# Attention scores from three bf16 parts instead of two float32r parts, with the 4-bit weight tables made during the attention

## The reference, cut to what matters

```
qkv = hidden_states @ Wqkv                     # 32 query heads of 16, one key head, one value head
scores = einsum('bqhd,bkd->bhqk', q, k) / 4 + slope[h] * (pos_k - pos_q)   # causal, else -1e30
attn = softmax(scores) @ v, then @ Wo
# feed-forward: gate, up (512 x 1376) and down (1376 x 512) are 4-bit codes:
w = scales[g_idx[k], n] * (code[k, n] - (zero[g_idx[k], n] + 1))
y = (silu(x @ gate) * (x @ up)) @ down
```

## Time and profile before

| | |
|---|---|
| median of 3 runs | 1397.24 us (1396.83 to 1401.67) |
| the profiled execution's own time | 1395.92 us |
| its span | 1394.1 us |
| mean granted clock of TensorE | 0.956 of full speed |
| busy: PE, weight loads, DVE, ACT, POOL | 1239.7, 826.8, 730.3, 571.8, 308.0 us |
| last instruction of the attention on POOL | issued at 747.83 us |
| first instructions of the feed-forward block | 753.37 us |
| first gate matmul | 799.73 us |

### The profile page before, as it was taken

How to read it: one execution, slowest core, us unless ns; L and a number is a source line. 1 busy time by engine, 2 the same in 40 slices (tenths; PEclk the granted TensorE clock), 3 DMA queues, 4 the chain that set the end, 5 groups by cost and what they waited for, 6 DMA issues and landing times. The chain is left out here.

```text
span 1394.1 us, 16630 instructions
## 1 busy us (share of the span) xinstructions
PE 1239.7 (89%) x6208; PEld 826.8 (59%) x6208; DVE 730.3 (52%) x1353; ACT 571.8 (41%) x1006; POOL 308.0 (22%) x329
## 2 busy tenths in 40 slices
PE   4599999999999999989992389999999999579995
PEld 4567456555554656544541257778778788346664
DVE  4376785786688887723214666342141210365553
ACT  5143455265456565556661344311111111034443
POOL 0121141111110101011124344411121111115554
PEclk9999999899999999999996599999999999889998
DMA  6534223201221012122001422230020010130303
GB/s 194 112 54 113 43 40 106 40 2 39 47 56 25 23 19 40 25 40 40 18 31 51 124 72 62 94 106 0 0 91 1 0 61 1 59 105 1 121 0 120
DMA packets 60942, 75.97 MB, mean 54 GB/s; under 512 B 14738, under 2 KB 37530, under 8 KB 60796
## 3 DMA queue, kind: packets, MB, share of 16 engines
q1 hardware_dynamic: 57252, 64.42, 18.7%
q0 software_dynamic: 2560, 8.39, 1.7%
q10 hardware_dynamic: 1056, 2.16, 0.4%
HBM read 53.46 MB, written 21.59 MB: 54 GB/s over the span
## 5 line engine op out<-in xcount | busy, mean ns | idle before, releaser
L792 DVE TENSOR_REDUCE mx<-bank 128x1 f32<-128x512 f32 (+2 forms) x576 | 367.3, 685 | 138.7 <-PE bank L910 85.1
L734 ACT ACTIVATE PT<-ST 128x512 f32<-128x512 f32 x576 | 313.3, 600 | 210.3 <-PE ST L975 90.0
L907 PE MATMUL bank<-KS,QS 126*128 126x512 f32 (+2 forms) x896 | 253.3, 365 | 18.1 <-DMA QS<-pos_scratch 15.8
L975 PE MATMUL ST<-QS,KS 128*128 128x512 f32 x576 | 240.1, 457 | 5.0 <-DMA QS<-mparts 4.1
L907 PEld LDWEIGHTS bank<-KS,QS 126*128 126x128 f32 x896 | 158.7, 197 | 82.9 <-DVE mx L792 37.7
L975 PEld LDWEIGHTS ST<-QS,KS 128*128 128x128 f32 x576 | 108.3, 195 | 82.6 <-ACT PT L734 64.1
L989 PE MATMUL PO<-PT,V 128*32 128x512 f32 x1152 | 152.2, 604 | 1.6 <-ACT PT L734 1.6
L51 PE MATMUL f_pair<-f_xT,gu 128*128 128x512 f32 (+1 forms) x352 | 142.1, 404 | 0.0
L1495 DVE TENSOR_TENSOR f_h<-f_h,f_pair 128x512 f32<-128x512 f32 (+1 forms) x44 | 30.2, 686 | 210.1 <-ACT f_h L1402 210.1
L53 PE MATMUL f_pair<-f_xT,gu 128*128 128x512 f32 (+1 forms) x352 | 139.8, 397 | 0.0
L52 PE MATMUL f_pair<-f_xT,gu 128*128 128x512 f32 (+1 forms) x352 | 139.4, 396 | 0.0
(11 more groups left out here) (181 smaller groups left out, 1777.6 us busy)
## 6 DMA issues: line engine op xcount, KB each, us to landing
QS<-q_scratch SPq DMA_DIRECT2D x48, 256.0 KB
q_scratch<-QP SPq DMA_DIRECT2D x24, 256.0 KB, 2.3
l_x<-x_dram SPq DMA_DIRECT2D x12, 512.0 KB, 4.2
xres<-_attn_hidden_states_dram POOLq DMA_DIRECT2D x16, 256.0 KB, 3.0
x_dram<-xout POOLq DMA_DIRECT2D x16, 256.0 KB, 2.4
f_xin<-x_dram SPq DMA_DIRECT2D x4, 1024.0 KB, 7.0
f_xsum<-x_dram SPq DMA_DIRECT2D x4, 1024.0 KB, 6.9
x_dram<-f_xsum SPq DMA_DIRECT2D x4, 1024.0 KB, 4.8
```

The costliest lines, as they stand in the source:

```text
L734: act.activation(PT[:, quad % PT_RING, n % 4, :], ST[:, n % ST_RING, :], ACT.Exp).then_inc(p_done, 1)
L792: v.tensor_reduce(mx[:, i % 2, z, h:h + m], at(u).rearrange("p (m k) -> p m k", m=m), AX.X, ALU.max).then_inc(bank_free_dve, 1)
L907: last = pe.matmul(at(u)[:, j * w:(j + 1) * w], hi(QS[0:ROWS1, slot, h + j, :]), hi(KS[b][0:ROWS1, k0:k0 + w]), start=(j == 0 or not diag) ...
L975: last = pe.matmul(dst, hi(KS[b][0:ROWS2, kb * P:(kb + 1) * P]), hi(QS[0:ROWS2, slot, h:h + 4, :]), start=True, stop=not diag)
```

## The change

Scores now come from bf16 operands. A float32 value is split in three bf16 parts; of the nine pairings six are kept (`Q_PART`, `K_PART`), so `KS` and `QS` hold 6 x 16 = 96 rows of parts, 6 rows of positions (key number split in two exact bf16 parts, slope in three), zeros, and 3 rows for three parts of the maxima. The two rows that subtracted slope times the block's first position, the same for a whole softmax row, are dropped. All of p1, tiles and masks are now bf16; projections, `values` and everything behind are as before. The second part is made by ACT from a float32 rest (`second_part`), the third on POOL for queries (`query_low`) and on DVE for keys and maxima (`keys_done`, `max_done`). The rest of a query tile lives in one of two halves of `qrest`, so DVE waits until POOL has read the one two tiles back. `q_scratch` is bf16 (runs of 256 bytes where they were 512), and a block's stack is six DMAs of half the size each. `k_scratch` and `pos_scratch` are gone. `PT` has five slots instead of three.

Second, `plan_order` gets work of its own for the feed-forward part from block 10 on: POOL clears and fetches table inputs (`clear_tables`, `fetch_tables`), DVE makes the tables and unpacks the first two code units, ACT splits the scales, PE turns the one-hot matrices ("dt"), and a sixth piece (`AFTER`) loads the first 512 rows of the attention's own output, normalizes and turns them into the `xT` that `ffn` uses. The buffers are laid out ahead in `program`. `ffn` starts with the six early pieces at once. The plan's costs change with it (`p1` and `tile` 232 to 218, new kinds of work, store and maxima delays longer).

```
-POS = slice(3 * HD, 3 * HD + 2)
-ROWS1 = P - 2
+PARTS = 3
+Q_PART = (0, 0, 0, 1, 1, 2)
+K_PART = (0, 1, 2, 0, 1, 0)
+SETS = len(Q_PART)
+POS = slice(SETS * HD, SETS * HD + 2 * PARTS)
+ROWS1 = P - PARTS
...
-PT_RING = 3
+PT_RING = 5
...
+AFTER = NC
+PIECES.append((0, 0, 4))
...
+            if u == maxima_of(AFTER_AT)[0]:
+                sp_issue(("load", AFTER), e)
+                pend["pool"].append((("clear",), e))
+                for k in range(CODE_RING):
+                    sp_issue(("codes", k), e)
...
-        q_scratch = nc.dram_tensor("q_scratch", (B, QB, 2, 4, HD, P // HD, P), F32).ap()
-        pos_scratch = nc.dram_tensor("pos_scratch", (1 + QB, 2, NH, P), F32).ap()
-        k_scratch = nc.dram_tensor("k_scratch", (ROWS2 - POS.start, S), F32).ap()
+        q_scratch = nc.dram_tensor("q_scratch", (B, QB, PARTS, 4, HD, P // HD, P), BF16).ap()
...
-        KS = [sb(f"KS{b}", [P, S]) for b in range(B)]
+        KS = [sb(f"KS{b}", [P, S], BF16) for b in range(B)]
-        QS = sb("QS", [P, QSLOTS, NH, P])
+        QS = sb("QS", [P, QSLOTS, NH, P], BF16)
+        mparts = sb("mparts", [NH, 2, PARTS, P], BF16)
...
-                for part, ready in enumerate((q_hi_done, q_lo_done)):
+                for part, ready in enumerate((q_hi_done, q_mid_done, q_lo_done)):
...
-                for g, part in enumerate((0, 0, 1)):
+                for g, part in enumerate(Q_PART):
-                sp.dma_start(QS[POS.stop:POS.stop + 2, slot, :, :], pos_scratch[qb]).then_inc(qs_in[slot], 16)
...
+                elif kind == "codes":
+                    if i == 0:
+                        full(sp, ("kv", NC - 1))
...
+            def query_low(k, m):
+                pool.wait_ge(q_mid_done, 4 * k + m + 1)
+                n = PIECES[k][2] * P
+                pool.tensor_tensor(QP[:, 2, m, cols_of(k)], qrest[:, m % 2, 0:n], QP[:, 1, m, cols_of(k)], ALU.subtract).then_inc(q_lo_done, 1)
+
+            def clear_tables():
+                full(pool, ("kv", NC - 1))
+                pool.wait_ge(q_out, Q_OUT * NC)
+                pool.memset(dq.zpacked, 0).then_inc(cleared, 1)
+                pool.memset(dq.s_raw, 0.0).then_inc(cleared, 1)
+                pool.memset(dq.tables, 0.0).then_inc(cleared, 1)
+                pool.memset(dq.ztab, 0.0).then_inc(cleared, 1)
+
+            def fetch_tables():
+                for dst, src in table_loads:
+                    pool.dma_start(dst, src, allow_slow_non_contiguous=True).then_inc(ids_in, 16)
+                pool.wait_ge(cleared, 4)
+                for m in range(3):
+                    g0, g, w = FIRST_GROUP[m], GROUPS_OF[m], D if m == 2 else INTER
+                    for i in range(3):
+                        pool.dma_start(dq.s_raw[i * G_ROWS + g0:i * G_ROWS + g0 + g, 0:w], mats[m][1]).then_inc(s_in, 16)
+                    pool.dma_start(dq.zpacked[g0:g0 + g, 0:w // PACK], mats[m][2]).then_inc(z_in, 16)
+
             piece_rstd(0)
...
+            def second_part(u):
+
+                kind, k = u[0][:-1], u[1]
+                freed(act, (kind, *u[1:]))
+                if kind == "q":
+                    m, n = u[2], PIECES[k][2] * P
+                    act.activation(QP[:, 1, m, cols_of(k)], qrest[:, m % 2, 0:n], ACT.Copy).then_inc(q_mid_done, 1)
+                elif kind == "kv":
+                    n = PIECES[k][2] * P
+                    act.activation(kpart[:, 1, 0:n], krest[:, 0:n], ACT.Copy).then_inc(k_mid_done, 1)
+                else:
+                    act.activation(mparts[:, k % 2, 1, :], mrest[:, k % 2, :], ACT.Copy).then_inc(m_mid_done, 1)
...
+                    if rest_before(u):
+                        _, kb, mb = rest_before(u)
+                        v.wait_ge(q_lo_done, 4 * kb + mb + 1)
+                    v.scalar_tensor_tensor(qrest[:, m % 2, 0:PIECES[k][2] * P], at(u)[:, 0:PIECES[k][2] * P], HD ** -0.5, QP[:, 0, m, cols_of(k)],
+                                           ALU.mult, ALU.subtract).then_inc(bank_free_dve, 1)
...
+            def keys_done(k):
+                b, t, n = PIECES[k]
+                v.wait_ge(k_mid_done, k + 1)
+                v.scalar_tensor_tensor(KS[b][0:SETS * HD, t * P:(t + n) * P], kpart[:, 1, 0:n * P], gmask[0:SETS * HD, 1:2], krest[:, 0:n * P],
+                                       ALU.mult, ALU.add).then_inc(ks_ready, 1)
+
+            def max_done(i):
+                v.wait_ge(m_mid_done, i + 1)
+                v.tensor_tensor(mparts[:, i % 2, 2, :], mrest[:, i % 2, :], mparts[:, i % 2, 1, :], ALU.subtract).then_inc(m_lo_done, 1)
...
-                    last = pe.matmul(at(u)[:, j * w:(j + 1) * w], hi(QS[0:ROWS1, slot, h + j, :]), hi(KS[b][0:ROWS1, k0:k0 + w]),
+                    last = pe.matmul(at(u)[:, j * w:(j + 1) * w], QS[0:ROWS1, slot, h + j, :], KS[b][0:ROWS1, k0:k0 + w],
...
+                elif kind == "dt":
+                    n = min(4, DQ_COLS - u[1])
+                    act.wait_ge(cleared, 4)
+                    act.activation(dq.onehotT[0:S_ROWS, u[1]:u[1] + n, :], at(u)[0:S_ROWS, 0:n * P].rearrange("p (u k) -> p u k", k=P),
...
-                last = pe.matmul(dst, hi(KS[b][0:ROWS2, kb * P:(kb + 1) * P]), hi(QS[0:ROWS2, slot, h:h + 4, :]), start=True, stop=not diag)
+                last = pe.matmul(dst, KS[b][0:ROWS2, kb * P:(kb + 1) * P], QS[0:ROWS2, slot, h:h + 4, :], start=True, stop=not diag)
...
-    uses = [("dq", 0, j) for j in EARLY_PIECES] + [("xt", 0, t) for t in range(4)]
+    uses = [("dq", 0, j) for j in EARLY_PIECES]
...
-            sp.dma_start(xin[:, :, :], rows(x1_dram, 0)).then_inc(x_in, 16)
-            sp.wait_ge(cleared, 2)
-            for m in range(3):
-                g0, g, w = FIRST_GROUP[m], GROUPS_OF[m], D if m == 2 else INTER
-                sp.dma_start(zpacked[g0:g0 + g, 0:w // PACK], mats[m][2]).then_inc(z_in, 16)
-                for i in range(3):
-                    sp.dma_start(s_raw[i * G_ROWS + g0:i * G_ROWS + g0 + g, 0:w], mats[m][1]).then_inc(s_in, 16)
-            sp.wait_ge(tables_done, 2)
-            for u in range(len(UNITS)):
-                load_codes(u)
-                if u == 2 * CODE_RING + 2:
-                    sp.wait_ge(turned, 4)
-                    sp.dma_start(xin[:, :, :], rows(x1_dram, 1)).then_inc(x_in, 16)
+            sp.dma_start(xin[:, :, :], rows(x1_dram, 1)).then_inc(x_in, 16)
+            for u in range(CODE_RING, len(UNITS)):
+                load_codes(sp, mats, dq, u)
...
-            for u in range(CODE_RING):
-                codes(u)
-            row_moments(0)
-            normalize(0)
...
-            pe.wait_ge(onehot_done, 1)
-            for a in range(DQ_COLS):
-                if a == 16:
-                    pe.wait_ge(onehotT_done, 1)
-                pe.matmul(turn[:, a // 4 % 4, a % 4 * P:(a % 4 + 1) * P], onehot[:, a, :], identb[:, :], start=True, stop=True).then_inc(onehot_turned, 1)
-            pe.wait_ge(onehotT_done, -(-DQ_COLS // 4))
-            pe.wait_ge(tables_done, 2)
             for j in EARLY_PIECES:
                 weight_piece(j)
-            for t in range(4):
-                transposes(0, t)
```

More of the change, by code:

```diff
@@ L10 @@
+from collections import namedtuple
 from contextlib import ExitStack
@@ L177, in sp_issue @@
             free["sp"] = t + 300
+        elif j[0] == "codes":
+            free["sp"] = t + 2400
+            end["codes", j[1]] = t + 6000
         else:
@@ L871, in _ @@
             v.wait_ge(consts_in, 32)
-            for u in FIRST:
+            for u in FIRST[:-1]:
                 take(u)
+            keys_done(0)
+            take(FIRST[-1])
             for u in ORDER["dve"]:
@@ L939, in fill @@
                         last = pe.transpose(dst[:, t * P:(t + 1) * P], kvf[:, t * P:(t + 1) * P], ident[:, :])
+                elif kind == "dt":
+                    pe.wait_ge(onehot_done, 1)
+                    for k in range(min(4, DQ_COLS - u[1])):
+                        last = pe.matmul(dst[0:S_ROWS, k * P:(k + 1) * P], dq.onehot[:, u[1] + k, :], identb[:, :], start=True, stop=True)
                 elif kind == "mt":
```

562 lines of the change are left out of this document (321 added, 241 removed).

## The result

The changed kernel takes **1317.36 us** (median of 4, 1314.54 to 1319.98) against 1397.75 of the kernel before, measured beside it: a ratio of **0.9419** (95% interval 0.9387 to 0.9452), about 81 us faster. The direction was right and the place of the hole too; the attention's share was sized at half of what it is. Rival 2, "all of it is realized", named 1316.

A forecast was written before the change was run, and what follows sets the result against it. PE was taken to bound the attention, DVE second, followed by a 46.4 us hole. Span 1394.1 - 24.5 (attention) - 29.6 (hole) = 1340.0 us, giving a forecast of 1343 us, range 1318 to 1372.

The forecast's parts named there:

- the hole: Between attention and first feed-forward gate matmul: 46.4 us shrinks to 16.8, -29.6 us, including a new 5.5 us wait for codes.
- the attention's share: Attention: -29.5 us from scores, plus 3 for its start and 2 for maxima, -24.5 us in all.
- Rival 2: All score savings realized, loads vanish wholly, deeper ring helps: 1316 us; chance 0.17 for below 1327 us.
- uncovered weight loads: Scores, behind 128-column masks and values quads: bf16 halves the exposed loads, 12.5 us saved, bounds nothing and 25.
- 128-key banks: Score segments of 128: a matmul falls from 0.103 to 0.07 us, 8.5 us saved, bounds 1.0 and 12.8.
- I take 80%: Attention: of 41.5 us PE savings 80% is realized, 33 us, as DVE rises above 90% and strict queues lose some.
- Rival 1: Attention: score gain eaten by DVE and new links, only the gap before feed-forward pays: 1370 us; chance 0.18.
- The additions: New work in the attention: 3.6 us on PE, 3 for longer chains at the start, 2 for maxima.
- block 1's first p1 near 73 us: Start of the attention: sign expected in the profile after, with longer chains adding 3 us, bounds -2 and 8.
- The ring: Attention: the deeper PT ring only loosens ACT while PE is full: 0 us, bounds -5 and 0.
- Rival 3: Query stores before blocks 0 and 1: shorter runs make stores take twice as long, 1348 us; chance 0.08.
- Rival 4: Attention: DVE waits for POOL at query rests and table steps, PE stops, slower, 1413 us; chance 0.04.

The follow-up runs named there:

- the streams: Extra unread matmul streams behind the last output projection, in the kernel before (float32r) and the changed kernel (bf16); for example 128 columns took 0.112 and 0.056 us.
- e1: Kernel before with bf16 score operands and nothing else (scores less accurate): 1335.57 us, ratio 0.9562.
- e8: Changed kernel with three of the six stack loads, and so three of the six products, left out: 1311.93 us, ratio 0.9365.
- e16: Changed kernel storing two of three query parts, the second used in place of the third: 1314.40 us, ratio 0.9396.
- e2: Kernel before with bf16 score operands and a PT ring of 5 instead of 3: 1332.08 us, ratio 0.9529.
- e15: e2 with the changed kernel's planner costs for score matmuls, normalization and store delays: 1337.73 us.
- e3: Changed kernel with a PT ring of 3 instead of 5: 1315.22 us, ratio 0.9405.

## Why the prediction was wrong

The step that failed is the term for **uncovered weight loads**, with the one for 128-key banks. I wrote "a bf16 load is half as long, so I take half of both: 12.5 us", bounds 0 and 25. By the streams the parts of the cycles and quads beyond the plain rate are 128 x (0.103 - 0.022) + 144 x (0.131 - 0.022) = 26.1 us: nearly all of it went, a little more than my upper bound of 25. What counts is whether the load still shows behind the columns ahead of it, not how much shorter it is. Only the mask of 128 leaves 0.008 uncovered (0.277 against 0.216 + 0.053). The 128-column term gave 14.3 instead of 8.5: I took 0.070, and the stream runs at 0.056, although its load is shown as 0.099 in the earlier trace rows; and the float32r stream runs at 0.112, not 0.103. (The price is the stream's; in place, with a 512-column mask between, it may be some 2 us less in all.) In the other direction 512 columns gave 0.011 instead of 0.016, 12.5 us with the diagonal tiles instead of 15.4, and 256 columns 3.1 instead of 5.1. The sum is 56 instead of 41.5, inside my bounds of 21.5 to 58 but far from my middle.

The second failed step is "I take 80%". PE's busy share in the middle is 98 to 99% at the new rate, with DVE at 84 or 90%, and `e1` shows the whole rate term in the time. Rival 1, which rests on the same fear, had 0.18 and should have had little.

The third had the other sign. The additions cost 16.4 us (677.18 to 693.59), where I had 3.6 for PE, 3 for the start and 2 for maxima. 7.3 are the planner's new costs, which I never priced. 7.0 are chains and stack loads (`e8` gives back 5.2 at the last projection, `e16` 2.0); the stacks of blocks 1 and 2 need 12 issues on SP, 5.49 us, which I had called "a few stack issues more". By luck two errors cancelled, an invented loss of 8 and 8 too little for the additions. What is left of the attention's miss, 46.1 instead of 24.5, is 15 us of rate, 5 of the wait at the start that `e1` shows, and 3.8 by which the trace of `e2` is shorter than `e1`'s, less 1.5 of a longer gap behind the last projection, to within 1 us.

**Start**: "block 1's first p1 near 73 us" was wrong: 69.29, and PE's wait fell from 9.94 us to 3.16. In the changed kernel the bytes don't explain it, as they do in `e1`: six loads of 128 KB are as much as three of 256. The order of work does. Kernel before, changed kernel, `e15`:

```profile
70.33 0.80 PE L907 MATMUL bank<-KS,QS 126*128 126x256 f32 x2 [9.94 <-DMA QS<-pos_scratch]
```

```profile
56.79 0.39 PE L1291 MATMUL ST<-QS,KS 128*128 128x512 bf16 x1
...
61.20 1.07 PE L1305 MATMUL PO<-PT,V 128*32 128x512 f32 x8
```

```profile
66.72 0.38 PE L907 MATMUL bank<-KS,QS 126*128 126x256 bf16 x2
```

With the new planner costs block 0's second pass stands ahead of block 1's first, from 56.79 to about 66 us, where PE had nothing to do before; in `e15`, which has that order and stacks of half the bytes, PE doesn't wait at all. I priced a longer chain in the old order, though the change gave the planner new delays. The stack itself lands 7.9 us behind its first issue (61.36 to 69.29) instead of 10.4 with as many bytes; why isn't shown. The wait cost more than its length: before, PE stood without matmuls from 60.4 us on and the granted clock is 0.50 from 66 to 73, also for the first matmuls behind the wait; in `e15` it is 1.00 from 56 to 75.

**The ring** at 0, bounds -5 and 0, was right within what the runs tell: `e2` shows 3.5, `e3` nothing.

**The hole** was right: the three pieces of old work went, the new wait was 5.13 us for 5.5, and the early pieces took 9.2 us for 11.3, so it ended 2.5 us better than said. The clock's quicker return, for which I added nothing, is in the last row of the table, 2.9 us, at most.

**Rival 3**: the stores of queries land after 2.0 us at 128 KB a part, in runs of 256 bytes, against 2.3 for 256 KB in runs of 512:

```profile
q_scratch<-QP SPq DMA_DIRECT2D x36, 128.0 KB, 2.0
```

Half the bytes take nearly the same time. That can be the shorter runs, or a fixed part of each landing, which no run here tells apart; but the landing wasn't later. The Trainium skill, "DMA: Bandwidth & Descriptors", section "Specifications", would have a read, modify and write here; no run shows a longer store by it.

**Rival 4**: before the block's end DVE's waits hold 1.7 us for POOL in all, at a `rstd`, and none at a `qrest` step. **Rival 2** had the time, but only one of its reasons: loads vanished all but wholly. The ring helped by 0 to 4 us, stack loads and order took back more than it allowed, and the better hole and the shorter start made up for it; that its 1316 is so near is in part luck.

## What to carry to other kernels

Price a matmul's operand type from cycles as they stand in the program, and for weights: where a matmul of another type or a short one stands in between, the float32r form paid 0.09 to 0.11 us each time here, and bf16 0.01 or less. An engine at 84 to 90% beside a full one needn't take a share of its gain. Where a planner writes the order, its costs are part of the change and have a price of their own: undo them alone once, even if the new ones are truer. And when a wait shrinks, look at what the engine does in its place before you thank the transfer.
